# Attention with the value products of each block in two parts of 256 query columns, one per step, buffers zeroed by VectorE and GpSimd, and no loops

## Chip, cores, metric

One core of one Trainium2 chip. The metric is the device time of one execution in microseconds (us); the median of several timed runs is compared. Engines are called TensorE (PE, its weight loads PEld), VectorE (DVE), ScalarE (ACT), GpSimd (POOL) and SyncE (SP, which issues DMAs).

## The reference

Two blocks over 8 x 1024 tokens of width 256, each `x = x + s * silu(g)` with `s` and `g` computed from a layer norm of `x`. The first is a state-space scan with a small fp8 product, the second a gated delta rule and a mixture of experts whose input is an attention. The change touches only that attention (16 heads of 8 features, each batch of 1024 tokens by itself):

```python
Q = (hs @ q_w + q_b).reshape(B, S, H, HD).transpose(0, 2, 1, 3)
K = (hs @ k_w + k_b).reshape(B, S, H, KPH).transpose(0, 2, 1, 3)
V = (hs @ v_w + v_b).reshape(B, S, H, KPH).transpose(0, 2, 1, 3)
scores = jnp.einsum('bhsk,bhtk->bhst', Q[..., :KPH], K) / math.sqrt(KPH)
attn = jax.nn.softmax(scores, axis=-1)
ao = jnp.einsum('bhst,bhtv->bhsv', attn, V)
```

## The kernel before

The program is a row of phases, each with its own buffers and its own instruction streams per engine: `ssm_inputs`, `ssm_scan`, `ssm_output`, `delta_inputs`, `delta_invert`, `delta_chunks`, `attention`, `experts`. A phase starts when the one before has ended. Only `attention` (line 2090) is changed.

The work of `attention` is cut into 32 units (`UNITS`), one for each batch `b` and each set `j` of four heads. A unit does three things for its four heads:

- maxima (`maxima`, line 2254): queries times keys with 128 queries on the partitions and 1024 keys in the free dimension, as two matmuls of 512 columns into one of two PSUM tiles `psM`. VectorE reduces each tile to minus its row maximum (`maximum`, L2395). There are 32 such tiles in a unit (`MT`). When they are there, `minus_max` (L2404, L2406) splits the maxima into a head and a rest, `turn` (L2273) transposes them on TensorE, ScalarE copies them to `topT` (L2355), and SyncE writes them by DMA into two more rows of the queries (`maxima_rows`, L2167). So the scores come out with the maximum already subtracted.
- scores (`scores`, L2280): the other way round, 128 keys on the partitions and 512 queries in the free dimension, 64 per unit (`BANKS`), each into one of three PSUM banks `psS`. ScalarE takes the exponential of each (`exponentials`, L2363) into a ring `probs` of 24 slots. A score waits until the exponential three entries earlier is done (`free`).
- values (`values`, L2293): for each 128 keys of the four heads one block of four products, 32 columns of the array each, 128 keys x 512 queries, all in fp32 and added up in one PSUM bank `psV` over the eight key tiles of a half of the queries. Each product shows as two load and two matmul records, so a block is eight of each. There are 16 blocks (`GROUPS`) per unit. VectorE copies `psV` out after eight of them (`collect`, L2411), and SyncE stores the sums.

TensorE's stream is written out by hand in steps; a unit has 32 (`step`). A step issues, in this order, the first half of a maxima tile, a score, the second half of the tile, a score. The maxima are those of the tile 8 steps ahead (`LEAD`) in the next unit. After every odd step `s` the whole block `s // 2 - 1` of values follows (`sequence`); two steps and their block are called a group here. Maxima and scores of one step use opposite halves of the array's rows. After score 52 (`TURN`) comes the transpose for the next unit. The TensorE, ScalarE and VectorE streams are already without loops; SyncE runs batches 0 to 6 in one loop, GpSimd batches 1 to 7.

At the start of the phase VectorE sets `ones` to one and then zeroes, for j = 0 to 3, `k4[j]` and `q4[j]`, then `top2`, before it takes up any maximum. SyncE loads unit j (17 DMAs) when its two buffers are zeroed, and after each the rows of ones. GpSimd sets `zeros` (of `Cleared`, which clears a table for a later phase), makes the identity and fills `v4`. TensorE then makes the 32 maxima tiles of unit 0 and 8 of unit 1 before the first step.

Of the kernel before, what the change touches and what calls it, by code (L numbers as in the profile page):

```python
# [2089 lines left out]
def attention(nc, A):  # L2090
# [18 lines left out]
    SLOTS, RING = 66, 24  # L2109


    at_slot = [n if n <= TURN else n + 1 for n in range(BANKS)]
    turn_entry = TURN + 1
    bank_at = dict(zip(at_slot, range(BANKS)))
    NE = BANKS + 1
    OPEN = 4
    COLLECTED = (18 + LEAD, FIRST + LEAD)
    with ExitStack() as ctx:
# [13 lines left out]
        ident_made, ready_made, filled = m.sem("ident_made"), m.sem("ready_made"), m.sem("filled")  # L2132
# [15 lines left out]
        with nc.Block() as block:  # L2148
            @block.sync
            def _(sp):  # L2150
# [10 lines left out]
                def maxima_rows(u, j, b):  # L2161

                    sp.wait_ge(act_done, u * NE + (turn_entry + 2 - NE) if not isinstance(u, int) or u else 1)
# [5 lines left out]
                def store(u, j, b, half):  # L2169
# [13 lines left out]
                maxima_rows(0, 0, 0)  # L2183

                def sequence(b, final):
                    for j in range(NQ):
                        u = b * NQ + j
                        store(u, j, b, 0)
                        if not (final and j == NQ - 1):
                            maxima_rows(u + 1, (j + 1) % NQ, b + (j + 1) // NQ)  # L2190
                        store(u, j, b, 1)
                        if not final:
                            load(b + 1, j)
                            cleared.store(sp, u)
# [11 lines left out]
            def _(pool):  # L2206
                cleared.make(pool)
# [3 lines left out]
                                   pattern=[[-1, P]], channel_multiplier=1).then_inc(ident_made, 1)  # L2211
                for j in range(NQ):
# [4 lines left out]

                def spread_values(b, j):
                    pool.wait_ge(loaded[j], b * 16 * LOADS + 16 * LOADS)
                    m.settle(pool)  # L2220
                    pool.tensor_copy(v4[j][:, :, :, 0:HD], vraw[j][:].rearrange("p c (h r) -> p c h r", r=HD)).then_inc(v_ready, 1)  # L2221

                for j in range(NQ):
                    spread_values(0, j)
                with pool.Fori(1, B) as b:
                    for j in range(NQ):
                        pool.wait_ge(summed, b * NQ * GROUPS + (j + 2 - NQ) * GROUPS)
                        spread_values(b, j)

            def slot(j, v):  # L2230
                return (j * SLOTS + v) % RING

            def steps():

                for s in range(FIRST, BANKS // 2 + FIRST):
                    yield s, s % (BANKS // 2), s // (BANKS // 2)

            @block.tensor
            def _(pe):
# [6 lines left out]
                def maxima(u, j, t, half):  # L2246

                    h, c = tile_of(t)
                    if half == 0:
                        if t > 1:  # L2250
                            pe.wait_ge(maxed, u * MT + (t - 1))
                        elif not isinstance(u, int) or u:
                            pe.wait_ge(maxed, u * MT + t - 1)
# [6 lines left out]
                def free(u, v):  # L2260
                    if v >= 3:
                        pe.wait_ge(act_done, u * NE + (v - 1))
# [989 lines left out]
```

## Time and profile before

| | us |
|---|---|
| median of 3 timed runs (lowest to highest) | 4021.08 (4018.24 to 4024.04) |
| the profiled execution | 3990.48 |
| its span, first to last instruction | 3988.9 |
| TensorE matmuls busy | 3377.5 |
| VectorE busy | 3155.0 |
| ScalarE busy | 2370.5 |
| GpSimd busy | 1366.7 |

The costliest groups of the page belong to the attention: 1024 maxima reductions on VectorE (L2395, 1205.1 us busy), 2048 exponentials (L2363, 1061.0 us), 2048 scores (L2280, 803.4 us), 2048 maxima matmuls (L2254, 704.9 us) and 4096 records of value matmuls (L2293, 546.3 us). The attention lies between about 1850 and 3276 us of the span. Busy times of different engines overlap. Those of TensorE hold modelled ends of matmuls. Idle time stands in brackets behind an instruction, with what released it; where several conditions had to be met, the one named is the last that the profile saw. In the order of time an entry "x4" merges neighbours of one kind on one engine.

### The profile page before, as it was taken

The page shows a single profiled execution, that of the slowest core. Times are in us where ns is not written, and L with a number is a line of the kernel's source. Part 1 is how long each engine was busy: PE and PEld are TensorE (multiplying, and loading weights), DVE is VectorE, ACT ScalarE, POOL GpSimd, SP SyncE. Part 2 cuts the span into 40 slices and gives each one's busy share as a digit, 9 for nine tenths or more (in the row PEclk, how much of TensorE's full clock was granted, in tenths as well). Part 3 has the DMA queues.
Part 4 walks back from the last instruction along what each step waited for, and adds up shares of the span by engine and source line. Part 5 has one row for each costly group of instructions (what it writes and reads, how often), then busy time and mean ns, then how long its engine had stood idle before and what let it go on. Part 6 is the DMA issues. An engine that isn't in the chain of part 4 may idle for free. (4 is left out here: it accounts for less than half of the span.)

```text
span 3988.9 us, 64991 instructions
## 1 busy us (share of the span) xinstructions
PE 3377.5 (85%) x19711; PEld 2058.5 (52%) x19712; DVE 3155.0 (79%) x4214; ACT 2370.5 (59%) x4325; POOL 1366.7 (34%) x953
## 2 busy tenths in 40 slices
PE   8969898996669799797999999999999976299950
PEld 6745455553458688795333333333333324189940
DVE  7869999997866566477899999999999935277868
ACT  6668888886955433210577777777777761033323
POOL 7859998994014454301000000000000005744520
PEclk9989999998889899997799999999999996599975
DMA  7854444544869632394122323223223115222258
GB/s 262 283 187 164 159 163 166 179 146 166 280 174 255 164 111 74 109 291 134 27 54 62 69 53 72 58 55 75 54 60 71 30 21 178 87 86 89 90 175 293
DMA packets 531451, 521.11 MB, mean 131 GB/s; under 512 B 84784, under 2 KB 441264, under 8 KB 531040
## 3 DMA queue, kind: packets, MB, share of 16 engines
q1 hardware_dynamic: 517248, 480.45, 41.0%
q0 software_dynamic: 13952, 37.74, 2.7%
q8 instruction: 106, 1.74, 0.2%
q14 instruction: 145, 1.19, 0.1%
HBM read 301.15 MB, written 215.71 MB: 130 GB/s over the span
## 5 line engine op out<-in xcount | busy, mean ns | idle before, releaser
L2395 DVE TENSOR_REDUCE at_top<-at_psM 128x1 f32<-128x1024 f32 x1024 | 1205.1, 1218 | 101.5 <-PE at_psM L2254 99.8
L2363 ACT ACTIVATE at_probs<-at_psS 128x512 f32<-128x512 f32 x2048 | 1061.0, 603 | 286.0 <-PE at_psS L2280 286.0
L2280 PE MATMUL at_psS<-at_q,at_k 64*128 64x512 f32 x2048 | 803.4, 471 | 8.2 <-ACT at_probs L2363 8.1
L2254 PE MATMUL at_psM<-at_k,at_q 62*128 62x512 f32 x2048 | 704.9, 454 | 41.3 <-DMA at_vraw<-scratch_vf 22.0
L655 POOL TENSOR_TENSOR sc_prod<-sc_state,sc_c_row 128x1024 f32<-128x1024 f32 x256 | 648.8, 2564 | 84.1 <-DVE sc_state L806 72.2
L2254 PEld LDWEIGHTS at_psM<-at_k,at_q 62*128 62x128 f32 x2048 | 313.1, 190 | 621.4 <-DVE at_top L2395 539.3
L806 DVE TENSOR_TENSOR_SCAN sc_state<-sc_dec,sc_psI 128x1024 f32<-128x1024 f32 x256 | 574.2, 2276 | 43.6 <-PE sc_psI L727 34.0
L2293 PE MATMUL at_psV<-at_probs,at_v 128*32 128x512 f32 x4096 | 546.3, 605 | 0.0
L738 PE MATMUL sc_psY<-sc_prod,sc_ident 128*128 128x512 f32 x1024 | 480.5, 599 | 15.2 <-DVE sc_y L792 15.2
L2221 POOL COPY at_v<-at_vraw 128x256 f32<-128x256 f32 x32 | 12.8, 401 | 1249.4 <-DMA at_vraw<-scratch_vf 1166.6
L2280 PEld LDWEIGHTS at_psS<-at_q,at_k 64*128 64x128 f32 x2048 | 337.7, 184 | 170.3 <-ACT at_probs L2363 160.4
L674 ACT ACTIVATE sc_scaled<-sc_uT,sc_b_col 128x256 f32<-128x256 f32 x768 | 325.2, 494 | 96.3 <-PE sc_psI L727 96.3
L688 ACT ACTIVATE sc_dec<-sc_dt,sc_a_exp 128x1024 f32<-128x1024 f32 x256 | 285.3, 1136 | 7.4 <-DVE sc_state L806 7.4
L727 PEld LDWEIGHTS sc_psI<-sc_ident,sc_scaled 128*128 128x128 f32 x1536 | 180.9, 144 | 177.0 <-DVE sc_state L806 82.8
L738 PEld LDWEIGHTS sc_psY<-sc_prod,sc_ident 128*128 128x128 f32 x1024 | 179.7, 192 | 167.1 <-issue 142.2
L727 PE MATMUL sc_psI<-sc_ident,sc_scaled 128*128 128x128 f32 x1536 | 207.9, 280 | 58.6 <-DVE sc_state L806 51.0
L2884 POOL DMA_INDIRECT scratch_ys<-ex_y,ex_slot x156 | 170.3, 1092 | 184.8 <-DVE ex_y L3017 137.5
L2438 PEld LDWEIGHTS ex_psY<-ek_w,ex_hid 128*128 128x128 f32 x1872 | 223.8, 188 | 3.2 <-issue 0.3
L2438 PE MATMUL ex_psY<-ek_w,ex_hid 128*128 x1872 | 224.9, 279 | 0.0
L2904 ACT ACTIVATE ex_xT<-ex_psT 128x512 fp32r<-128x512 f32 x39 | 23.3, 598 | 266.4 <-PE ex_psT L2934 266.4
L2580 POOL DMA_INDIRECT scratch_xs<-er_rows,ek_spot x128 | 130.5, 1019 | 74.5 <-issue 41.3
L2293 PEld LDWEIGHTS at_psV<-at_probs,at_v 128*32 128x32 f32 x4096 | 80.6, 108 | 128.4 <-ACT at_probs L2363 94.1
(409 smaller groups left out, 4904.4 us busy)
## 6 DMA issues: line engine op xcount, KB each, us to landing
sc_c_row<-scratch_bc SPq DMA_DIRECT2D x128, 512.0 KB, 3.7
scratch_xs<-at_zeros SPq DMA_DIRECT2D x140, 264.0 KB, 4.7
sc_b_row<-scratch_bc SPq DMA_DIRECT2D x32, 512.0 KB, 5.0
ec_y<-scratch_ys SPq DMA_DIRECT2D x32, 512.0 KB, 6.1
ex_x<-scratch_xs SPq DMA_DIRECT2D x39, 264.0 KB, 3.3
si_x<-in_x SPq DMA_DIRECT2D x16, 512.0 KB, 5.6
scratch_xn<-si_xn SPq DMA_DIRECT2D x16, 512.0 KB, 6.2
scratch_x_t<-si_xT SPq DMA_DIRECT2D x16, 512.0 KB, 3.1
```

The source lines that it names most:

```text
L655: pool.tensor_tensor(prod[:, (n * H + h) % 8, :], state[slot][:], c_row[n % ROWS][:], ALU.mult).then_inc(prod_ready, 1)
L674: act.activation(scaled[DIAG.index(n) % 2][:, c, :, :], uT[k][:, c, :, :], ACT.Copy, scale=b_col[:, bass.ds(b * CHUNKS + c, 1), n]).then_i ...
L688: act.activation(dec[slot][:], dt[k][h][:], ACT.Exp, scale=a_exp[:, h, n:n + 1]).then_inc(dec_ready, 1)
L727: last = pe.transpose(psI[h][:, c, :], scaled[order % 2][:, c, h, :], ident[:])
L738: last = pe.matmul(psY[h][:, cols], ident[:], prod[:, own % 8, cols], start=(n == 0), stop=(n == S - 1))
L806: dve.tensor_tensor_scan(state[slot][:], dec[slot][:], psI[h][:].rearrange("p c t -> p (c t)"), 0.0, ALU.mult, ALU.add).then_inc(state_rea ...
L2254: ins = pe.matmul(psM[t % 2][:, half * TILE:(half + 1) * TILE], rows_of(q4[j], h, 0, MAXROW)[:, c * P:(c + 1) * P], rows_of(k4[j], h, 0, M ...
L2280: pe.matmul(psS[v % 3][:], rows_of(k4[j], h, 0, GROUP)[:, c * P:(c + 1) * P], rows_of(q4[j], h, 0, GROUP)[:, half * TILE:(half + 1) * TILE ...
L2293: last = pe.matmul(psV[32 * h:32 * h + 32, :], v4[j][:, c, h, :], probs[:, slot(j, at_slot[4 * g + n]), :], start=(c == 0), stop=(c == KC ...
L2363: act.activation(probs[:, slot(j, v), :], psS[v % 3][:], ACT.Exp).then_inc(act_done, 1)
L2395: dve.tensor_reduce(top[j % 2][:, h, c:c + 1], psM[t % 2][:], AX.X, ALU.max, negate=True).then_inc(maxed, 1)
L2438: last = pe.matmul(out, a, b, start=start and n == 0, stop=stop and n == len(parts) - 1)
```

## The change

Value products: `values` now takes a group number and a part. Part 0 is query columns 0 to 255 of the block, part 1 columns 256 to 511. After an odd step comes part 0 of the block whose turn it is, after the even step behind it part 1. For the last block of each half (`last_keys`) both parts come after the odd step. The flag that starts an accumulation is set only on part 0 of the first key tile, for both parts lie in the same bank. Only part 1 tells ScalarE and VectorE that the block is done.

Zeroing: VectorE zeroes `k4`, `q4` of units 0 and 1, then sets `ones` and `top2`, and waits for `top2` alone; GpSimd zeroes those of units 2 and 3 first, and `zeros` is set after the first four `spread_values`. The loads wait for `zeroed[j]` only; the rows of ones are stored after all four loads.

No loops: SyncE's and GpSimd's batches are written out, and entries of the score banks are numbered once over all units (`score_at`, `turn_at`); bank and ring slot follow from that number.

```diff
-    SLOTS, RING = 66, 24
+    RING, PART = 24, TILE // 2
+    score_at, turn_at, entries = {}, {}, 0
+    turn_at[0], entries = entries, entries + 1
+    for u in range(UNITS):
+        for s in range(MT):
+            for n in (2 * s, 2 * s + 1):
+                score_at[u, n], entries = entries, entries + 1
+                if n == TURN and u + 1 < UNITS:
+                    turn_at[u + 1], entries = entries, entries + 1
...
                 for j in range(NQ):
-                    sp.wait_ge(ready_made, 2 * j + 3)
+                    sp.wait_ge(zeroed[j], 2)
                     m.settle(sp)
                     load(0, j)
+                sp.wait_ge(ones_made, 1)
+                m.settle(sp)
+                for j in range(NQ):
                     for group in range(2):
                         dst = k4[j][GROUP * group + MAXROW:GROUP * (group + 1), :, :].bitcast(F32)
                         sp.dma_start(dst, ones[:]).then_inc(ones_in, 16)
...
-                with sp.Fori(0, B - 1) as b:
-                    sequence(b, False)
-                sequence(B - 1, True)
+                for u in range(UNITS):
+                    store(u, 0)
+                    if u + 1 < UNITS:
+                        maxima_rows(u + 1)
+                    store(u, 1)
+                    if u + NQ < UNITS:
+                        load(u // NQ + 1, u % NQ)
+                        cleared.store(sp, u)
...
             def _(pool):
-                cleared.make(pool)
+                for j in range(2, NQ):
+                    pool.memset(k4[j][:].bitcast(F32), 0.0).then_inc(zeroed[j], 1)
+                    pool.memset(q4[j][:].bitcast(F32), 0.0).then_inc(zeroed[j], 1)
...
                 for j in range(NQ):
                     spread_values(0, j)
-                with pool.Fori(1, B) as b:
+                cleared.make(pool)
+                for b in range(1, B):
...
-                def values(u, j, g):
+                def values(group, part):
 
-                    half, c = g // KC, g % KC
-                    pe.wait_ge(act_done, u * NE + (at_slot[4 * g + 3] + 2))
-                    if c == 0:
-                        pe.wait_ge(sums_ready, u * NHALF + (half + 1))
-                    if g == 0:
-                        pe.wait_ge(v_ready, u + (2 * NQ + 1))
+                    u, g = group // GROUPS, group % GROUPS
+                    j, half, c = u % NQ, g // KC, g % KC
+                    cols = slice(part * PART, (part + 1) * PART)
+                    if part == 0:
+                        pe.wait_ge(act_done, score_at[u, 4 * g + 3] + 1)
+                        if c == 0:
+                            pe.wait_ge(sums_ready, u * NHALF + (half + 1))
+                        if g == 0:
+                            pe.wait_ge(v_ready, u + (2 * NQ + 1))
                     for n, h in enumerate(KEYED):
-                        last = pe.matmul(psV[32 * h:32 * h + 32, :], v4[j][:, c, h, :], probs[:, slot(j, at_slot[4 * g + n]), :],
-                                         start=(c == 0), stop=(c == KC - 1))
-                    last.then_inc(summed, 1)
+                        last = pe.matmul(psV[32 * h:32 * h + 32, cols], v4[j][:, c, h, :], probs[:, slot(u, 4 * g + n), cols],
+                                         start=(c == 0 and part == 0), stop=(c == KC - 1 and part == 1))
+                    if part == 1:
+                        last.then_inc(summed, 1)
+
+                def values_after(at):
+
+                    group = (at - 3) // 2
+                    if group < 0:
+                        return
+                    last_keys = group % KC == KC - 1
+                    if at % 2:
+                        values(group, 0)
+                    if at % 2 == 0 and not last_keys or at % 2 and last_keys:
+                        values(group, 1)
...
+                for u in range(UNITS):
+                    for s in range(MT):
+                        if u and s == 0:
+                            pe.wait_ge(top_in[u % NQ], (u // NQ + 1) * 16 * QUAD)
+                        step(u, s)
+                        values_after(u * MT + s)
+                for at in range(UNITS * MT, UNITS * MT + 2):
+                    values_after(at)
...
             def _(dve):
-                dve.memset(ones[:], 1.0).then_inc(ready_made, 1)
-                for j in range(NQ):
-                    dve.memset(k4[j][:].bitcast(F32), 0.0).then_inc(ready_made, 1)
-                    dve.memset(q4[j][:].bitcast(F32), 0.0).then_inc(ready_made, 1)
-                dve.memset(top2[:], 0.0).then_inc(ready_made, 1)
+                for j in range(2):
+                    dve.memset(k4[j][:].bitcast(F32), 0.0).then_inc(zeroed[j], 1)
+                    dve.memset(q4[j][:].bitcast(F32), 0.0).then_inc(zeroed[j], 1)
+                dve.memset(ones[:], 1.0).then_inc(ones_made, 1)
+                dve.memset(top2[:], 0.0).then_inc(top2_made, 1)
```

## Rows read from the trace of the kernel before

**Rows 1.** Table by stage: stretch, length, busy time per engine (instructions), TensorE clock, DMA.
```profile
1960.00:3200.00 1240.00, 1233.61 (x7582) 446.03 (x7582) 1149.82 (x1064) 981.70 (x1918) 11.22 (x28) 1.00 0.26 60
```

**Rows 2.** Order of time, one group: start us, us, engine, line, operation, [idle before].
```profile
2401.40 0.50 PE L2280 MATMUL at_psS<-at_q,at_k 64*128 64x512 f32 x1
...
2401.73 0.73 PE L2280 MATMUL at_psS<-at_q,at_k 64*128 64x512 f32 x2
2401.93 2.06 ACT L2363 ACTIVATE at_probs<-at_psS 128x512 f32<-128x512 f32 x4 [0.55 <-PE at_psS L2280]
...
2401.97 0.72 PE L2254 MATMUL at_psM<-at_k,at_q 62*128 62x512 f32 x2
...
2402.16 2.36 DVE L2395 TENSOR_REDUCE at_top<-at_psM 128x1 f32<-128x1024 f32 x2 [0.25 <-PE at_psM L2254]
...
2402.58 0.18 PEld L2280 LDWEIGHTS at_psS<-at_q,at_k 64*128 64x128 f32 x1 [0.33 <-ACT at_probs L2363]
...
2403.01 0.16 PEld L2293 LDWEIGHTS at_psV<-at_probs,at_v 128*32 128x32 f32 x8 [0.25 <-ACT at_probs L2363]
...
2404.01 0.49 PE L2280 MATMUL at_psS<-at_q,at_k 64*128 64x512 f32 x1
```

**Rows 3.** Groups by line: count, busy us, mean ns, idle before (1900 to 3300 us).
```profile
L2363 ACT ACTIVATE at_probs<-at_psS 128x512 f32<-128x512 f32 x2048 | 1061.0, 603 | 286.0 <-PE at_psS L2280 286.0
```

**Rows 4.** Order of time, last unit, TensorE: two groups in a row.
```profile
3249.78 0.73 PE L2280 MATMUL at_psS<-at_q,at_k 64*128 64x512 f32 x3
...
3252.38 0.73 PE L2280 MATMUL at_psS<-at_q,at_k 64*128 64x512 f32 x3
```

**Rows 5.** Line 2273, the transposes: duration min/median/max, first and last start.
```profile
L2273 PE MATMUL at_psS<-at_ident,at_top x32: 328/329/332, 1962.9 to 3265.8; 128*128 128x128 f32 x32
```

**Rows 6.** Line 2293, the value products: loads and matmuls, min/median/max ns.
```profile
L2293 PEld LDWEIGHTS at_psV<-at_probs,at_v x4096: 106/109/151, 1931.4 to 3273.5; 128*32 128x32 f32 x196
L2293 PE MATMUL at_psV<-at_probs,at_v x4096: 592/617/1061, 1931.4 to 3274.0; 128*32 128x512 f32 x196
```

**Rows 7.** Line 1997 of an earlier stage: loads and matmuls of 256 columns.
```profile
L1997 PEld LDWEIGHTS dc_psOut<-dc_wo,dc_og x128: 186/190/190, 1704.8 to 1845.3; 128*128 128x128 f32 x128
L1997 PE MATMUL dc_psOut<-dc_wo,dc_og x128: 379/379/483, 1704.8 to 1845.5; 128*128 128x256 f32 x128
```

**Rows 8.** Order of time, earlier stage: line 1997, eight matmuls in one row.
```profile
1797.53 1.99 PE L1997 MATMUL dc_psOut<-dc_wo,dc_og 128*128 128x256 f32 x8
```

**Rows 9.** Order of time, the step with the transpose.
```profile
2424.91 0.50 PE L2280 MATMUL at_psS<-at_q,at_k 64*128 64x512 f32 x1
...
2425.34 0.33 PE L2273 MATMUL at_psS<-at_ident,at_top 128*128 128x128 f32 x1
...
2425.60 0.49 PE L2254 MATMUL at_psM<-at_k,at_q 62*128 62x512 f32 x1
...
2426.44 0.39 PE L2280 MATMUL at_psS<-at_q,at_k 64*128 64x512 f32 x1
2426.76 0.16 PEld L2293 LDWEIGHTS at_psV<-at_probs,at_v 128*32 128x32 f32 x8 [0.31 <-ACT at_probs L2363]
```

**Rows 10.** Order of time, the start of the attention.
```profile
1853.32 1.76 DVE L2386 MEMSET at_ones<- 2x2048 f32 x1 [6.10 <-PEq L3207]
...
1855.46 1.76 DVE L2388 MEMSET at_k<- 128x2048 f32 x1 [0.38 <-issue]
...
1858.03 0.95 POOL L2213 MEMSET at_v<- 128x1024 f32 x1
...
1859.47 0.36 SPq L2156 DMA_DIRECT2D at_q<-scratch_qs  x1
...
1867.86 0.53 PEld L2254 LDWEIGHTS at_psM<-at_k,at_q 62*128 62x128 f32 x4 [22.36 <-issue]
...
1872.39 2.36 DVE L2395 TENSOR_REDUCE at_top<-at_psM 128x1 f32<-128x1024 f32 x2
...
1926.56 0.79 PE L2254 MATMUL at_psM<-at_k,at_q 62*128 62x512 f32 x1 [4.33 <-DMA at_q<-at_topT]
```

More of the change, by code:

```diff
@@ L2244, in tile_of, with maxima @@
                     return HEADS[t % QUAD], t // QUAD
[L2246 to L2253, printed above, removed]
+                def maxima(u, t, half):
+                    j, (h, c) = u % NQ, tile_of(t)
+                    if half == 0 and u * MT + t > 1:
+                        pe.wait_ge(maxed, u * MT + t - 1)
                     ins = pe.matmul(psM[t % 2][:, half * TILE:(half + 1) * TILE],
@@ L2258, in maxima @@
                         ins.then_inc(scored, 1)
-                def free(u, v):
-                    if v >= 3:
-                        pe.wait_ge(act_done, u * NE + (v - 1))
-                    elif v < 2 and (not isinstance(u, int) or u):
-                        pe.wait_ge(act_done, u * NE + v)
-                    elif isinstance(u, int) and not u:
-                        pe.wait_ge(act_done, 1)
-                def turn(u, needed):
-                    free(u, turn_entry)
-                    if needed:
-                        top_at.wait(pe, u + 1, "rest")
-                    pe.transpose(psS[turn_entry % 3][:, 0:P], top2[:], ident[:]).then_inc(keyed, 1)
@@ L2275, in scores, with free, turn @@
-                def scores(u, j, n):
+                def free(e):
+                    if e >= 3:
+                        pe.wait_ge(act_done, e - 2)
+                def turn(u):
+                    e = turn_at[u]
+                    free(e)
+                    top_at.wait(pe, u, "rest")
+                    pe.transpose(psS[e % 3][:, 0:P], top2[:], ident[:]).then_inc(keyed, 1)
+                def scores(u, n):
+                    j, e = u % NQ, score_at[u, n]
                     half, c, h = n // (KC * QUAD), n // QUAD % KC, KEYED[n % QUAD]
-                    v = at_slot[n]
-                    free(u, v)
-                    pe.matmul(psS[v % 3][:], rows_of(k4[j], h, 0, GROUP)[:, c * P:(c + 1) * P],
+                    free(e)
+                    pe.matmul(psS[e % 3][:], rows_of(k4[j], h, 0, GROUP)[:, c * P:(c + 1) * P],
@@ L2313, in _ @@
-                pe.wait_ge(loaded[0], 16 * LOADS)
-                for t in range(MT):
-                    for half in range(NHALF):
-                        maxima(0, 0, t, half)
-                pe.wait_ge(loaded[1], 16 * LOADS)
-                for t in range(LEAD):
-                    for half in range(NHALF):
-                        maxima(1, 1, t, half)
-                top_at.wait(pe, 0, "rest")
-                pe.transpose(psS[2][:, 0:P], top2[:], ident[:]).then_inc(keyed, 1)
+                        scores(u, n)
@@ L2323, in _ @@
+                        if n == TURN and u + 1 < UNITS:
+                            turn(u + 1)
+                for u, count in ((0, MT), (1, LEAD)):
+                    pe.wait_ge(loaded[u], 16 * LOADS)
+                    for t in range(count):
+                        for half in range(NHALF):
+                            maxima(u, t, half)
+                turn(0)
                 pe.wait_ge(top_in[0], 16 * QUAD)
                 pe.wait_ge(ones_in, 2 * 16 * NQ)
-                for s in range(FIRST):
-                    step(0, 0, 0, s, False, False)
@@ L2377, in _, with turned @@
[L2377 to L2382 removed]
+                def turned(u):
+                    e = turn_at[u]
+                    act.wait_ge(keyed, e + 1)
+                    act.activation(topT[:], psS[e % 3][:, 0:P], ACT.Copy).then_inc(act_done, 1)
@@ new lines, in exponential @@
+                def exponential(u, n):
+                    e, at = score_at[u, n], u * BANKS + n
+                    act.wait_ge(keyed, e + 1)
+                    if at >= RING:
+                        act.wait_ge(summed, (at - RING) // QUAD + 1 + GROUPS)
+                    act.activation(probs[:, slot(u, n), :], psS[e % 3][:], ACT.Exp).then_inc(act_done, 1)
+                turned(0)
+                for u in range(UNITS):
+                    for s in range(MT):
+                        for n in (2 * s, 2 * s + 1):
+                            exponential(u, n)
+                            if n == TURN and u + 1 < UNITS:
+                                turned(u + 1)
```

137 lines of the change are left out of this document (35 added, 102 removed).

## The prediction

> **What bounds the kernel now.** I read the views from the outside in. The stage table says where the attention stands: between 1960 and 3200 us TensorE is busy for 1233.6 of 1240 us, VectorE for 1149.8, ScalarE for 981.7, at full granted clock [rows 1]. A busy TensorE proves little, because the ends of its matmuls are modelled and pairs that wait look busy, and VectorE is nearly as full. So I went to the order of time within one group, which is two steps: four pairs of matmuls (maxima and scores on opposite halves of the array's rows, so they run together), then one block of value products.
>
> The group's first score starts at 2401.40, that of the next at 2404.01: 2.61 us [rows 2]. In between the last of the four scores waits until 2402.58, and the releaser named is ScalarE. The chain that fixes the period: first score at 1.40; its exponential at 1.93, 0.53 later; it takes 0.60 [rows 3]; 0.05 later, at 2.58, the score starts that needs this same bank (there are three); the value block follows 0.43 later, at 3.01; it holds TensorE for 1.00, and at 4.01 the next group starts [rows 2]. 0.53 + 0.60 + 0.05 + 0.43 + 1.00 = 2.61. VectorE idles 0.25 per period, ScalarE 0.55, because the long block keeps new scores away [rows 2]. That VectorE is not the limit shows in the last unit: it has no maxima at all, and its period is still 2.60 (3249.78 to 3252.38) [rows 4]. A whole unit of 16 groups takes (3265.8 - 1962.9)/31 = 42.03 us, from the first and the last of the 32 transposes [rows 5].
>
> **The change: the value products.** Each block is cut into 256 columns at the odd step and 256 at the next even step, except the last block of each half (2 of 16), which stays whole so that its sum is collected at the same step. The number of instructions of line 2293 doubles from 4096 to 8192, with the same number of columns.
>
> What is a half block worth? A whole one holds TensorE for 4.01 - 3.01 = 1.00 [rows 2], in two rounds of four matmuls side by side. The shortest matmul of 512 columns there takes 592 ns [rows 6]; one of the same type with 256 columns, on line 1997, takes 379 [rows 7]. So 256 columns less save 213 ns: the stream scales, the rest (about 0.17) is latency. A half block saves 0.213 in each of its two rounds: 1.00 - 0.43 = 0.57. Its lower bound is 0.50, if everything scaled. Its upper bound: each round's weight load stands bare, 0.109 more per half block, [rows 6], thus 0.68. I take 0.57, for line 1997 runs eight 256-column matmuls, each with a load of 190 ns [rows 7], in 1.99 us, so (1.99 - 0.38)/7 = 0.23 apart [rows 8]: loads longer than these hide under the same stream.
>
> The step then runs: first pair at 0, second pair 0.33 later (1.40 to 1.73) [rows 2]; from the second pair, when it did not wait, to the first load of the block 0.32 (2426.44 to 2426.76, the one place where a block follows an unstalled score) [rows 9]; half block 0.57. Sum 1.22 to 1.23 a step, 2.45 a group. Are the waits gone? First score of a step to its exponential's end 1.13, plus 0.05: 1.18 after it the next step's second score may start, and it is due at 1.22 + 0.33 = 1.55. The loop of before with the half block is 1.18 + 0.43 + 0.57 = 2.18 for two steps, below 2.45. ScalarE wants two exponentials, 0.52 each when they follow one another (2.06 for four): 1.03 a step. VectorE wants at most 1.18 (2.36 for two); a maximum starts 0.43 behind its second matmul (1.73 to 2.16), so at 0.76 in its step, and frees its bank at about 2.0, which the step two on needs at 2.44 [rows 2]. So every wait has cover, the thinnest 0.04 a step on VectorE, and what is late next is TensorE itself: the forecast is a step bound by the array.
>
> The two whole blocks: second pair at 0.33, block from 0.65 to 1.65, then a step with no block (0.33 + 0.23, as from 1.73 to 1.97 [rows 2]), next pair at 2.21; its second score waits for the exponential of the step before: 1.65 + 1.18 = 2.83 instead of 2.55, and the following block then starts at 3.26. From block to block 2.61, as before. The transpose of line 2273 takes 0.43 behind the first pair and 0.26 ahead of the second (2424.91, 2425.34, 2425.60) [rows 9], and the block then comes 0.43 after that fresh pair: 1.12 where a plain step has 0.65, so 0.47. Before, the group with the transpose took 0.24 more, since part of it lay in the waits.
>
> Unit: 14 x 2.45 + 2 x 2.61 + 0.47 = 40.0 us against 42.03, so 2.0 less; for 32 units (the last has the same chain) 65 us. With the ends for the half block: 0.50 would give 28 x 0.07 = 2 us more per unit but then VectorE is the limit, and its busy time is 1149.8/1240 x 42.03 = 39.0 per unit [rows 1], so at most 1 us more, 32 in all; 0.68 would cost 28 x 0.11 = 3.1 per unit, 99 in all.
>
> **The change: the start of the stage.** VectorE now zeroes two buffers' pairs instead of four; GpSimd the others; the ones come after. Before: the ones (1853.32, 1.76) stood ahead of the first pair, so SyncE issued its first load at 1859.47 and the first maxima matmul ran at 1867.86; and VectorE took up the maxima only at 1872.39, behind ten memsets [rows 10]. One memset with its gap is 2.15 (1853.32 to 1855.46). Now the first load starts 2.15 earlier, the first matmul at 1865.7, and VectorE is free at 1872.4 - 4 x 2.15 = 1863.8, so the first maximum waits for the matmuls: some 0.9 behind the first, an estimate from the 0.79 of one at this low clock (at 1926.56), at 1866.6: 5.8 us earlier [rows 10]. Behind it the chain is as before, 40 maxima. GpSimd's four memsets, at twice 0.95 for twice the columns, last until about 1861; the identity follows, before 1865; the value buffers, needed after 1930, come behind it. That both engines write at once costs nothing: VectorE's memset takes 1.76 while GpSimd writes too [rows 10]. The last two loads wait on GpSimd, but SyncE first issues the two groups ahead of them, 17 issues of 0.36 each, so it comes to them at about 1857.3 + 12.3 = 1869.6.
>
> **The change: no loops.** Only SyncE and GpSimd had loops. Their work has cover: at the start TensorE waits 4.33 us from the transpose until the rows of topT have landed (1926.56) [rows 10], and within the units the transpose comes 5 steps and 1.7 us, that is 7.8 us, ahead of need. I cost it at nothing, with 0 to 2 us either way; if that cover were gone each of the 31 units would wait.
>
> **Sum.** 65 + 5.8 = 71 us. The profiled execution took 3990.5 us with a span of 3988.9; the median of the timed runs, 4021.1, is 0.8% above it. The same 71 us are taken off the median: 3950.
>
> **A rule against it.** The trace shows all eight weight loads of a block within 0.16 us [rows 2], while the first round's matmuls, 617 ns long in the median, are running [rows 6]. The Trainium skill (TensorE: Matmul & The Clock Gate, Part 3, what overlaps and what doesn't) says a weight load overlaps a running matmul only when the row groups differ; here every value product uses all rows, so by it the second round's loads would stand bare in each half block. The trace of before disagrees. It is the mechanism of the first rival.
>
> **The rivals.** (1) Slower: the fixed part of a half block is larger than scaling says, because the second round's loads no longer hide, at 0.109 [rows 6]. Then a step is 0.65 + 0.68 = 1.335 and a unit 28 x 1.335 + 5.22 + 0.47 = 43.07: 1.04 x 32 = 33 slower, less 5.8 at the start, 4048. It decides from a half block of 0.65 on, where a unit is 42.0 again; my 0.57 is only 0.08 below. For it: the margin is thin and is paid 896 times. Against: line 1997's spacing. Chance 0.08. (2) No change in the steps: TensorE still waits for an exponential or a maximum once per group and 2.61 stays; only the start gains: 4015. For it: three banks are few. Against: the covers above, and the last unit, where only ScalarE's loop is left. Chance 0.07. (3) Part of the gain: VectorE, which will be busy 39 of 40 us, falls behind after each collection of psV (twice a unit) and at the two subtractions, and TensorE, in order, waits; up to 0.4 each time, 1 us a unit, 32 in all: 3965 to 3985. Chance 0.13. (4) VectorE's bound is reached, the steps being shorter than I add up: 3915 to 3925. Chance 0.05. The forecast keeps 0.67, from 3930 to 3965.
>
> The range holds the forecast and (3), with the little of (4) that lies above its lower end: 3925 to 3985, 0.80. A measurement of this kernel tells about 0.2% (8 us) from no change. Faster by more than that: the forecast, (3), (4), and 0.02 of (2), where the waits shrink by a little, 0.87 in all; within it the rest of (2), 0.05; slower (1), 0.08.
>
> **What would show it.** Right: 128x256 matmuls of the value line at about 379 ns in the second round; steps of 1.22 us from maxima pair to maxima pair; transposes 40.0 us apart; ScalarE's idle time ahead of the exponentials cut to half or less; TensorE's waits for ScalarE only behind the whole blocks; the first maximum near 1866.6. Wrong: half blocks over 0.65 (rival 1), maxima waits of TensorE that last over 0.3 us beyond the block (rival 3), or a group of 2.61 with a wait for ScalarE in it (rival 2).

## The result, and the profile after

| | before | after |
|---|---|---|
| median of the timed runs, us | 4020.51 (4 runs, 4018.24 to 4024.04) | 3953.51 (4 runs, 3952.32 to 3954.11) |
| ratio, 95% interval | | 0.9832 [0.9815, 0.9849] |
| span of the profiled execution, us | 3988.9 | 3952.5 |

The median fell by 67 us. The prediction was 3950 us, 71 less than the median that it started from.

Table by stage, the kernel after: stretch, length, then busy time (instructions) of PE, PEld, DVE, ACT, POOL, TensorE's granted clock, DMA share, GB/s.

```profile
1970.00:3150.00 1180.00, 1179.99 (x11319) 455.13 (x11321) 1168.64 (x1058) 1022.36 (x1911) 11.27 (x28) 1.00 0.28 63
```

VectorE was busy for 92.7% of the stage [rows 1]; it is now for 99.0%. That number alone would say that VectorE is the bound, and experiment 6 shows that it isn't. VectorE's busy time reads high: the record of one maximum lasts 1.22 us, but two in a row take 2.36 [rows 2], so the next can begin 1.14 us behind the one before it.

Order of time in the kernel after, two plain steps; it answers to [rows 2].

```profile
2400.95 0.49 PE L2251 MATMUL at_psM<-at_k,at_q 62*128 62x512 f32 x1
2400.95 0.18 PEld L2273 LDWEIGHTS at_psS<-at_q,at_k 64*128 64x128 f32 x1
2400.95 0.49 PE L2273 MATMUL at_psS<-at_q,at_k 64*128 64x512 f32 x1
...
2401.28 0.39 PE L2251 MATMUL at_psM<-at_k,at_q 62*128 62x512 f32 x1
2401.29 0.39 PE L2273 MATMUL at_psS<-at_q,at_k 64*128 64x512 f32 x1
2401.49 2.32 ACT L2353 ACTIVATE at_probs<-at_psS 128x512 f32<-128x512 f32 x4 [0.37 <-PE at_psS L2273]
2401.61 0.16 PEld L2289 LDWEIGHTS at_psV<-at_probs,at_v 128*32 128x32 f32 x8 [0.36 <-issue]
2401.61 0.64 PE L2289 MATMUL at_psV<-at_probs,at_v 128*32 128x256 f32 x8
2402.18 0.18 PEld L2251 LDWEIGHTS at_psM<-at_k,at_q 62*128 62x128 f32 x1 [0.41 <-DVE at_top L2375]
2402.18 0.49 PE L2251 MATMUL at_psM<-at_k,at_q 62*128 62x512 f32 x1
...
2402.52 0.39 PE L2273 MATMUL at_psS<-at_q,at_k 64*128 64x512 f32 x1
2402.84 0.16 PEld L2289 LDWEIGHTS at_psV<-at_probs,at_v 128*32 128x32 f32 x8 [0.36 <-issue]
```

No score waits here any more. The step is 2402.18 - 2400.95 = 1.23: 0.34 from one score to the next (2401.29), 0.32 to the block, 0.57 for the half block. The wait for VectorE that the row at 2402.18 names is idle time of the weight loads while the half block's matmuls still ran. With maxima half as long (experiment 6) the same gap of 0.41 stands at the same place, so VectorE doesn't make it.

The places where something still waits are the groups with a whole block. Order of time in the kernel after, behind such a block:

```profile
2410.00 0.50 PE L2273 MATMUL at_psS<-at_q,at_k 64*128 64x512 f32 x1
2410.24 0.68 DVE L2389 COPY at_sums<-at_psV 128x512 f32<-128x512 f32 x1
...
2411.18 0.18 PEld L2273 LDWEIGHTS at_psS<-at_q,at_k 64*128 64x128 f32 x1 [0.42 <-ACT at_probs L2353]
...
2411.61 0.64 PE L2289 MATMUL at_psV<-at_probs,at_v 128*32 128x256 f32 x8
```

From the first score behind the whole block (2410.00) to the one that waits (2411.18) it is 1.18, the 0.53 + 0.60 + 0.05 of the prediction. Between 1970 and 3150 us a score's load waited for an exponential 58 times, which is twice a unit, once for each whole block.

Groups by line in the kernel after (mean ns; idle time and what ended it):

```profile
L2375 DVE TENSOR_REDUCE at_top<-at_psM 128x1 f32<-128x1024 f32 x1024 | 1229.4, 1222 | 22.1 <-PE at_psM L2251 19.1
L2353 ACT ACTIVATE at_probs<-at_psS 128x512 f32<-128x512 f32 x2048 | 1108.9, 596 | 177.4 <-PE at_psS L2273 54.8
```

The value products in the kernel after (duration min/median/max, first and last start), to set beside [rows 6]:

```profile
L2289 PE MATMUL at_psV<-at_probs,at_v x8192: 379/379/634, 1928.9 to 3210.8; 128*32 128x256 f32 x200
```

ScalarE idled 286.0 us ahead of its exponentials [rows 3], now 177.4, of which the view puts 54.8 down to a score. The matmuls of 256 columns take 379 ns, as line 1997's did [rows 7].

The transposes within the units, first and last start (this answers to [rows 5]):

```profile
L2266 PE MATMUL at_psS<-at_ident,at_top x31: 328/329/331, 1958.0 to 3162.6; 128*128 128x128 f32 x31
```

A unit takes (3162.6 - 1958.0)/30 = 40.15 us, against 42.03. The difference times 32 is 60 us.

The start of the stage in the kernel after, order of time (answers to [rows 10]):

```profile
1855.96 1.76 DVE L2366 MEMSET at_k<- 128x2048 f32 x1 [6.13 <-PEq L3181]
...
1859.97 0.36 SPq L2160 DMA_DIRECT2D at_q<-scratch_qs  x1
...
1868.57 0.53 PEld L2251 LDWEIGHTS at_psM<-at_k,at_q 62*128 62x128 f32 x4 [20.46 <-issue]
...
1869.90 1.23 DVE L2375 TENSOR_REDUCE at_top<-at_psM 128x1 f32<-128x1024 f32 x1 [3.48 <-PE at_psM L2251]
```

From VectorE's first memset to its first maximum it was 1872.39 - 1853.32 = 19.07 us, now 13.94: 5.1 less. With the units that makes 65 us, and the timed medians differ by 67.

The two profiled executions differ by 36 us only, for a reason outside the attention. In the execution profiled before, the phase behind it (routing and the experts' products) ran from 3291.1 to 3852.7; in the one after, from 3227.8 to 3816.2: 561.6 and 588.4 us. The row of an early and of a late instruction, first of before, then of after:

```profile
L2708 DVE TENSOR_SCALAR er_obw<-er_ones,er_ob x2: 279/279/279, 3291.1 to 3291.3; 128x128 f32<-128x128 f32 x2
L3146 DVE SCALAR_TENSOR_TENSOR ec_shift<-ec_known x1: 226/226/226, 3852.7 to 3852.7; 128x64 f32<-128x64 f32 x1
```

```profile
L2682 DVE TENSOR_SCALAR er_obw<-er_ones,er_ob x2: 281/281/281, 3227.8 to 3228.0; 128x128 f32<-128x128 f32 x2
L3120 DVE SCALAR_TENSOR_TENSOR ec_shift<-ec_known x1: 226/226/226, 3816.2 to 3816.2; 128x64 f32<-128x64 f32 x1
```

The eleven runs below have edits in the attention only, and in their profiled executions this stretch took 585.0 to 597.4 us (597.4, from 3277.8 to 3875.2, in `before_max_half`, which is the kernel before with one edit). So the execution of the kernel before that was profiled was 23 to 36 us short there, and it lay 28 us below the fastest timed run of its kernel (3990.5 against 4018.2). Below, kernels are compared by their units and stages where a single execution is all there is.

### The profile page after: what moved, and what is told of

It reads as the page before. It is cut to its first block and busy times, and to the rows that moved or that the text cites. A ratio compares the mean times of both kernels' runs of the same rounds, so it can differ in the third digit from the quotient of the medians.

```text
span 3952.5 us, 71732 instructions
## 1 busy us (share of the span) xinstructions
PE 3330.8 (84%) x23806; PEld 2070.5 (52%) x23807; DVE 3174.8 (80%) x4210; ACT 2420.0 (61%) x4324; POOL 1370.9 (35%) x957
## 5 line engine op out<-in xcount | busy, mean ns | idle before, releaser
L2375 DVE TENSOR_REDUCE at_top<-at_psM 128x1 f32<-128x1024 f32 x1024 | 1229.4, 1222 | 22.1 <-PE at_psM L2251 19.1
L2353 ACT ACTIVATE at_probs<-at_psS 128x512 f32<-128x512 f32 x2048 | 1108.9, 596 | 177.4 <-PE at_psS L2273 54.8
L2251 PE MATMUL at_psM<-at_k,at_q 62*128 62x512 f32 x2048 | 756.1, 453 | 29.6 <-DMA at_vraw<-scratch_vf 20.1
L2273 PE MATMUL at_psS<-at_q,at_k 64*128 64x512 f32 x2048 | 756.5, 446 | 0.9 <-ACT at_probs L2353 0.9
L2289 PE MATMUL at_psV<-at_probs,at_v 128*32 128x256 f32 x8192 | 641.2, 390 | 0.0
L2289 PEld LDWEIGHTS at_psV<-at_probs,at_v 128*32 128x32 f32 x8192 | 167.8, 108 | 349.1 <-issue 175.5
L2273 PEld LDWEIGHTS at_psS<-at_q,at_k 64*128 64x128 f32 x2048 | 309.0, 185 | 43.7 <-ACT at_probs L2353 42.5
```

What stands on the lines that cost most here:

```text
L2251: ins = pe.matmul(psM[t % 2][:, half * TILE:(half + 1) * TILE], rows_of(q4[j], h, 0, MAXROW)[:, c * P:(c + 1) * P], rows_of(k4[j], h, 0, M ...
L2273: pe.matmul(psS[e % 3][:], rows_of(k4[j], h, 0, GROUP)[:, c * P:(c + 1) * P], rows_of(q4[j], h, 0, GROUP)[:, half * TILE:(half + 1) * TILE ...
L2289: last = pe.matmul(psV[32 * h:32 * h + 32, cols], v4[j][:, c, h, :], probs[:, slot(u, 4 * g + n), cols], start=(c == 0 and part == 0), sto ...
L2353: act.activation(probs[:, slot(u, n), :], psS[e % 3][:], ACT.Exp).then_inc(act_done, 1)
L2375: dve.tensor_reduce(at, psM[t % 2][:], AX.X, ALU.max, negate=True).then_inc(maxed, 1)
```

## The experiments

My theory: before, a group lasts as long as the chain of its first score, that score's exponential, the fourth score that needs the bank, and the whole block (2.61 us). Half blocks shorten the chain below TensorE's own work, and TensorE's own work sets the step after. The rivals: VectorE is the bound before or after; narrow matmuls or straight code bring the gain; the narrow matmuls cost bare weight loads.

**1. The block whole again, everything else kept** (`whole_odd`).

```diff
-    RING, PART = 24, TILE // 2
+    RING, PART = 24, TILE
...
-                                         start=(c == 0 and part == 0), stop=(c == KC - 1 and part == 1))
-                    if part == 1:
-                        last.then_inc(summed, 1)
+                                         start=(c == 0), stop=(c == KC - 1))
+                    last.then_inc(summed, 1)
...
                     if at % 2:
                         values(group, 0)
-                    if at % 2 == 0 and not last_keys or at % 2 and last_keys:
-                        values(group, 1)
```

> The changed kernel, but each block whole (512 columns) behind the odd step, as before; zeroing and straight code stay. My theory: the chain first score, exponential, fourth score, block returns, with a group of 2.61 us and transposes 42.0 us apart; only the start of the stage gains, some 5 us: 4015 us, ratio to before 0.999. Rival (straight code on SyncE and GpSimd brought part of the gain): 3955 to 4000.

Measured: 4016.7 us, ratio 0.9984 [0.9975, 0.9994]. Its transposes:

```profile
L2266 PE MATMUL at_psS<-at_ident,at_top x31: 327/328/332, 1957.3 to 3218.3; 128*128 128x128 f32 x31
```

(3218.3 - 1957.3)/30 = 42.03 us a unit, as before. What is left is the start: from VectorE's first memset to its first maximum it takes 1867.02 - 1853.02 = 14.00 us, as in the change. The written-out loops bring nothing in the units; nearly all of the gain is in the value products.

**2. Both halves behind the odd step** (`two_parts_odd`): as narrow and as many as in the change, but not moved.

```diff
                     if at % 2:
                         values(group, 0)
-                    if at % 2 == 0 and not last_keys or at % 2 and last_keys:
                         values(group, 1)
```

> The changed kernel with both halves of each block behind the odd step, so the matmuls are as narrow and as many as in the change, but not moved. My theory: what pays is that a block no longer stands in one piece ahead of the next scores; two halves together take 1.00 to 1.02 us, so a group 2.61 to 2.63 us: 4015 to 4025. Rival (narrow matmuls are better by themselves): near 3953. Rival (each narrow round costs something): 1024 more rounds at 0.109 at most, 4100 or more.

Measured: 4017.9 us, ratio 0.9993 [0.9983, 1.0003]; a unit takes (3220.6 - 1956.5)/30 = 42.14 us.

```profile
L2266 PE MATMUL at_psS<-at_ident,at_top x31: 327/328/332, 1956.5 to 3220.6; 128*128 128x128 f32 x31
```

Narrowness brings nothing by itself and costs 0.1 us a unit. What pays is the place of the second half.

**3. The zeroing as before** (`old_zeroing`).

```diff
-                for j in range(2):
+                dve.memset(ones[:], 1.0).then_inc(ones_made, 1)
+                for j in range(NQ):
                     dve.memset(k4[j][:].bitcast(F32), 0.0).then_inc(zeroed[j], 1)
                     dve.memset(q4[j][:].bitcast(F32), 0.0).then_inc(zeroed[j], 1)
-                dve.memset(ones[:], 1.0).then_inc(ones_made, 1)
```

and without GpSimd's four memsets.

> The changed kernel with the zeroing as before: VectorE sets ones and then all eight buffers. My theory: steps unchanged (transposes 40.15 us apart), the first maximum some 5 us later, so 3958 us. Rival (the zeroing is covered anyway): 3953.

Measured: 3960.5 us, ratio 0.9842 [0.9826, 0.9859]. The intervals overlap, so the ratios can't tell this from the change's 0.9832. The trace can: from VectorE's first memset to its first maximum it takes 1872.12 - 1853.06 = 19.06 us, 5.1 more than in the change, and the units last (3165.6 - 1961.0)/30 = 40.15, as there. Both parts of the new zeroing are undone at once here; what each is worth was not tried.

```profile
1853.06 1.76 DVE L2362 MEMSET at_ones<- 2x2048 f32 x1 [6.11 <-PEq L3178]
...
1872.12 2.36 DVE L2372 TENSOR_REDUCE at_top<-at_psM 128x1 f32<-128x1024 f32 x2
```

**4. The kernel before with half of each exponential** (`before_exp_half`).

```diff
-                    act.activation(probs[:, slot(j, v), :], psS[v % 3][:], ACT.Exp).then_inc(act_done, 1)
+                    act.activation(probs[:, slot(j, v), 0:TILE // 2], psS[v % 3][:, 0:TILE // 2], ACT.Exp).then_inc(act_done, 1)
...
                 dve.memset(top2[:], 0.0).then_inc(ready_made, 1)
+                dve.memset(probs[:, :, TILE // 2:], 1.0).then_inc(ready_made, 1)
```

> The kernel before, with each exponential taken over 256 of its 512 columns (the other half of each slot is set to one at the start, which costs VectorE some 5 us, so the values of half of the queries are left out). My theory: the exponential is in the chain of 2.61 us, so a group gets shorter by what the exponential does, 0.2 us, until VectorE binds at 2.36: 2.40 us, unit 38.6, in all 110 us less (3915). Rival (TensorE's amount of work or VectorE is the bound before): group stays at 2.61, 4025.

Measured: 3963.2 us, beside 4023.4 for the kernel before, where I had expected 3915; a unit takes (3203.6 - 1965.3)/31 = 39.94. Order of time, one plain group, then a later place where VectorE copies `psV` out:

```profile
2400.07 0.49 PE L2280 MATMUL at_psS<-at_q,at_k 64*128 64x512 f32 x1
...
2400.60 1.36 ACT L2363 ACTIVATE at_probs<-at_psS 128x256 f32<-128x256 f32 x4 [1.00 <-PE at_psS L2280]
...
2401.03 0.18 PEld L2280 LDWEIGHTS at_psS<-at_q,at_k 64*128 64x128 f32 x1
...
2402.47 0.50 PE L2280 MATMUL at_psS<-at_q,at_k 64*128 64x512 f32 x1
...
2415.62 0.68 DVE L2412 COPY at_sums<-at_psV 128x512 f32<-128x512 f32 x1
...
2416.42 0.16 PEld L2293 LDWEIGHTS at_psV<-at_probs,at_v 128*32 128x32 f32 x8 [0.24 <-ACT at_probs L2363]
...
2419.28 0.16 PEld L2293 LDWEIGHTS at_psV<-at_probs,at_v 128*32 128x32 f32 x8 [0.37 <-issue]
```

A plain group lasts 2402.47 - 2400.07 = 2.40 us. The chain with the exponential now 0.38 says the same: 0.53 + 0.38 + 0.05 + 0.43 + 1.00 = 2.39. ScalarE's work was far from full in the kernel before (981.7 of 1240 us [rows 1]), and yet a shorter exponential shortens the group. The unit did not become 38.6. With groups of 2.40, VectorE, which needs 2.28 for two maxima that follow one another at 1.14, has little time to catch up after its two copies of `psV` and its subtractions, and TensorE waits for it: from block to block behind the copy it is 2419.28 - 2416.42 = 2.86 us. I had left those out.

**5. The kernel before with half of each maximum** (`before_max_half`).

```diff
-                    dve.tensor_reduce(top[j % 2][:, h, c:c + 1], psM[t % 2][:], AX.X, ALU.max, negate=True).then_inc(maxed, 1)
+                    dve.tensor_reduce(top[j % 2][:, h, c:c + 1], psM[t % 2][:, 0:TILE], AX.X, ALU.max, negate=True).then_inc(maxed, 1)
```

> The kernel before, with each maximum over 512 of the 1024 keys. My theory: VectorE was not the bound, so a group stays at 2.61 and a unit at 42.0; the 40 maxima before the first step save some 12 us, as they did in the changed kernel, 4009 in all. Rival (VectorE's 0.25 idle per group was its own doing): a unit of 40 or less.

Measured: 4012.9 us beside 4022.5; a unit takes (3252.7 - 1951.4)/31 = 41.98.

```profile
L2273 PE MATMUL at_psS<-at_ident,at_top x32: 328/329/332, 1951.4 to 3252.7; 128*128 128x128 f32 x32
```

VectorE, busy for 93% of the stage, was not the bound before.

**6. The changed kernel with half of each maximum** (`after_max_half`), by the same edit.

> The changed kernel, with each maximum taken over 512 of the 1024 keys (any value near the maximum serves the softmax, so this leaves out half of VectorE's work and little else). My theory: a step of 1.23 us is TensorE's own (pair 0.33, second pair to block 0.32, half block 0.57), so transposes stay 40.15 us apart; only the 40 maxima before the first step get faster, some 20 us: 3933. Rival (VectorE, busy 39 of 40 us, holds TensorE back): transposes nearer than 39.5.

Measured: 3949.4 us beside 4021.5; a unit takes (3149.2 - 1944.4)/30 = 40.16.

```profile
L2266 PE MATMUL at_psS<-at_ident,at_top x31: 328/329/331, 1944.4 to 3149.2; 128*128 128x128 f32 x31
```

and one maximum in the order of time:

```profile
2399.46 0.69 DVE L2375 TENSOR_REDUCE at_top<-at_psM 128x1 f32<-128x512 f32 x1 [0.90 <-PE at_psM L2251]
```

VectorE's maxima take 0.69 and it now idles between them, and the unit moves by no more than a hundredth. So VectorE doesn't set the step, and with experiment 7, where ScalarE doesn't either, TensorE's own work is left. I had expected 3933. From VectorE's first memset to the first transpose of the units it takes 1944.4 - 1854.8 = 89.6 us, against 1958.0 - 1856.0 = 102.0 in the change: the start gained 12 us and not my 20. The granted clock is 0.50 there, and VectorE now waits for the matmuls of each two tiles, which come 2.00 us apart where two maxima took 2.36:

```profile
1886.62 1.29 DVE L2375 TENSOR_REDUCE at_top<-at_psM 128x1 f32<-128x512 f32 x2 [0.71 <-PE at_psM L2251]
1888.62 1.29 DVE L2375 TENSOR_REDUCE at_top<-at_psM 128x1 f32<-128x512 f32 x2 [0.71 <-PE at_psM L2251]
```

Of these 12 us 7 were lost again in the phase behind the attention (595.7 us here, 588.4 in the change's execution).

**7. The changed kernel with half of each exponential** (`after_exp_half`), the edit of experiment 4.

> The changed kernel, with each exponential taken over 256 of its 512 columns (values of half of the queries left out; setting the other half to one costs some 5 us at the start). My theory: the plain steps stay at 1.23; only behind the two whole blocks of a unit does a score wait for an exponential, so each of these groups goes from 2.62 to about 2.45 and a unit from 40.15 to 39.8: 3947. Rival (the exponential is still in the chain of every group, as before, where the same edit took 0.21 off each): unit 37 to 38.

Measured: 3956.5 us beside 4021.5; a unit takes (3159.9 - 1959.9)/30 = 40.00 instead of 40.15. The same edit that took 2.1 us from a unit before takes 0.15 after: the exponential is out of the chain everywhere but behind the whole blocks. There it gave 0.08 each where I had said 0.17. The group itself fell to 2.41 us from block to block (2409.21 to 2411.62), but the step behind it took 1.36 and not 1.23, since its maxima wait for VectorE, which works off maxima without a pause behind its copy of `psV`:

```profile
2411.05 5.74 DVE L2376 TENSOR_REDUCE at_top<-at_psM 128x1 f32<-128x1024 f32 x5
...
2412.32 0.18 PEld L2251 LDWEIGHTS at_psM<-at_k,at_q 62*128 62x128 f32 x1 [0.55 <-DVE at_top L2376]
```

**8. Quarters** (`quarters`): each half block as two runs of 128 columns.

```diff
-                    for n, h in enumerate(KEYED):
-                        last = pe.matmul(psV[32 * h:32 * h + 32, cols], v4[j][:, c, h, :], probs[:, slot(u, 4 * g + n), cols],
-                                         start=(c == 0 and part == 0), stop=(c == KC - 1 and part == 1))
+                    for quarter in (2 * part, 2 * part + 1):
+                        cols = slice(quarter * P, (quarter + 1) * P)
+                        for n, h in enumerate(KEYED):
+                            last = pe.matmul(psV[32 * h:32 * h + 32, cols], v4[j][:, c, h, :], probs[:, slot(u, 4 * g + n), cols],
+                                             start=(c == 0 and quarter == 0), stop=(c == KC - 1 and quarter == 3))
```

> The changed kernel with each half block made in two runs of 128 columns: the same columns, twice as many matmuls and loads again. My theory: a matmul of 128 columns still hides the next loads (0.107 us of stream against 0.109), so a half block stays at 0.57 to 0.62: unit 40.2 to 41.5, 3955 to 3995. Rival (my first in the prediction: loads stand bare as the matmuls get shorter): 0.109 for each of two more rounds, step 1.45, unit 46, 4140.

Measured: 3966.8 us beside 4021.5; a unit takes (3168.3 - 1957.3)/30 = 40.37, that is 0.21 more, or 8 ns for each of its 28 half blocks. Two of its rows, a block and the pair behind it:

```profile
2402.00 0.64 PE L2290 MATMUL at_psV<-at_probs,at_v 128*32 128x128 f32 x16
2402.57 0.50 PE L2251 MATMUL at_psM<-at_k,at_q 62*128 62x512 f32 x1
```

Sixteen matmuls of 128 columns hold TensorE for 0.57 us, as eight of 256 do. The loads stay hidden even here. Of the 13 us between 3966.8 and 3953.5 the units make 7. The phase behind the attention took 594.1 us here and 588.4 in the change's execution, which is most of the rest.

**9. Parted by heads** (`by_heads`): two heads at all 512 columns in each part.

```diff
-                    for n, h in enumerate(KEYED):
-                        last = pe.matmul(psV[32 * h:32 * h + 32, cols], v4[j][:, c, h, :], probs[:, slot(u, 4 * g + n), cols],
-                                         start=(c == 0 and part == 0), stop=(c == KC - 1 and part == 1))
+                    for n, h in list(enumerate(KEYED))[2 * part:2 * part + 2]:
+                        last = pe.matmul(psV[32 * h:32 * h + 32, :], v4[j][:, c, h, :], probs[:, slot(u, 4 * g + n), :],
+                                         start=(c == 0), stop=(c == KC - 1))
```

> The changed kernel with the blocks parted by heads, not by queries: two heads at 512 columns in each part, so as many matmuls as before in all. My theory: four heads run side by side, and two take as long as four, so a part holds TensorE for 1.00 and not for 0.57: step 1.65, unit near 54, 4390 us. Rival (any part of half the products takes half the time, so that spreading alone pays): step 1.23, 3953.

Measured: 4324.1 us beside 4021.5; a unit takes (3516.3 - 1965.1)/30 = 51.71.

```profile
2400.14 1.05 PE L2289 MATMUL at_psV<-at_probs,at_v 128*32 128x512 f32 x4
2401.12 0.49 PE L2251 MATMUL at_psM<-at_k,at_q 62*128 62x512 f32 x1
```

Two heads hold TensorE for 0.98 us, as long as four do, because the four run side by side. The step is 1.64, where I had said 1.65. A group with a whole block takes 2.61 as elsewhere; my unit of 54 had given each of the two 1 us more.

**10. Values in bfloat16, parted and whole** (`bf16_values` on the change, `bf16_whole` on experiment 1).

```diff
-        v4 = [m.sb(f"v4{j}", [P, KC, QUAD, 32]) for j in range(NQ)]
+        v4 = [m.sb(f"v4{j}", [P, KC, QUAD, 32], BF16) for j in range(NQ)]
...
-        probs = m.sb("probs", [P, RING, TILE])
+        probs = m.sb("probs", [P, RING, TILE], BF16)
```

> The changed kernel with the exponentials and the values in bfloat16 (less exact: the value products are made once instead of in two rounds, at one column per cycle). My theory: TensorE's step falls below VectorE's, half block 0.25 and step 0.90, so VectorE binds: 32 maxima at 1.14, two copies and the two subtractions, 38.1 to 38.6 us a unit, 3890 to 3905. Rival (TensorE's fixed times or ScalarE at 1.03 a step hold it): unit 39 or more.

> As bf16_values, but with each block whole behind the odd step, as before the change. My theory: a whole block is then 0.36 long, the chain first score, exponential, fourth score, block takes 0.53 + 0.60 + 0.05 + 0.43 + 0.36 = 1.97, less than VectorE's 2.36, so parting the block brings nothing more: within 5 us of bf16_values. Rival (parting is worth 66 us by itself): 3950 or more.

Measured: parted 3942.6 us, ratio 0.9804 [0.9766, 0.9843]; whole 3904.6 us, ratio 0.9719 [0.9695, 0.9744]. I had expected 3890 to 3905 for the parted version and the whole one within 5 us of it. So parting does not just bring nothing here, it costs 38 us, which neither side had foreseen. Tables by stage, parted; the first three are stretches of different granted clock, the last is the stage:

```profile
1966.50:1986.90 20.40, 16.56 (x144) 6.95 (x142) 20.40 (x20) 19.03 (x36) 0.40 (x1) 1.00 0.54 122
1986.90:2007.30 20.40, 20.40 (x109) 8.81 (x109) 16.95 (x17) 14.63 (x28) 0.00 (x0) 0.50 0.01 3
2027.90:2034.70 6.80, 6.78 (x36) 2.95 (x36) 6.03 (x7) 4.85 (x10) 0.00 (x0) 0.50 0.05 11
1950.00:3150.00 1200.00, 1019.97 (x7744) 432.03 (x7743) 1153.16 (x1084) 1050.57 (x1963) 11.27 (x28) 0.89 0.27 62
```

and the stage of the whole version:

```profile
1950.00:3100.00 1150.00, 893.52 (x5770) 361.60 (x5768) 1134.05 (x1077) 1037.40 (x1943) 11.21 (x28) 0.97 0.27 64
```

At full clock VectorE binds, busy for 20.40 of 20.40 us with 20 instructions; TensorE idles a fifth of the time. After such a stretch its granted clock is 0.50, here for 20 us, the 1.2 GHz level, and then TensorE is busy all the time and gets through 109 matmul records where there were 144. From the first transpose of the units to the last, the parted version has 35 such slow stretches, most of them under 7 us, 251 us in all; the whole version has 15, 58 us in all. An estimate from these rows: 193 us more at the low level, with a quarter less done (109 for 144), cost some 47 us, so the clock is enough to explain the 38. In the parted version the stage's mean clock is 0.89, in the whole version 0.97; a unit takes 39.75 and 38.47 us. Why the parted version has more of the slow stretches is not settled: it spreads the same columns over more and shorter pauses, but no run separates the two, and it is the whole version whose TensorE is idle more (893.5 of 1150 us busy against 1020.0 of 1200). The mechanism expected (VectorE becomes the bound near 38.1 to 38.6 us a unit) shows in the whole version. The rival for the parted one (39 us or more) had the size right and the reason wrong: it named TensorE's fixed times or ScalarE.

`bf16_whole` is faster than both kernels, by the ratios some 45 us below the change. It is less exact in the exponentials and values, so it trades exactness for time, which the change does not.

## Why the prediction was right

- The bound of before: right. The chain of 2.61 us is confirmed by experiment 4, where a group went to 2.40 as the exponential got shorter. That VectorE was not the bound is confirmed by experiment 5.
- A half block 0.57: measured 0.57. The 592 to 379 ns scaling and line 1997's spacing carried it. Rival 1 (bare loads, 0.109 for each half block) fell; experiment 8 shows loads hidden even at 128 columns: all eight loads of a half block issue within 0.16 us, and two more rounds cost 8 ns and not 218. The Trainium skill (TensorE: Matmul & The Clock Gate, Part 3) says that a load overlaps running matmuls only when the row groups differ; this case's trace goes against it. The same Part also names loads into the background weight buffer as ones that are pulled ahead; no run here tells whether these were such.
- The step 1.22 to 1.23: measured 1.23. Whole-block groups 2.61: measured (40.15 - 28 x 1.23 - 0.47)/2 = 2.62. The transpose's step: the pair 0.26 behind it and the block 0.43 behind that pair, as taken (below).
- A unit 40.0: measured 40.15. Nearly all of the 0.15 is the rounding of the step, 1.23 instead of 1.225, over 28 steps.
- The units in sum 65: measured 60, for the same reason. The start 5.8: measured 5.1. Counted from VectorE's first memset, the first maxima matmul came 1.9 us earlier (12.61 for 14.54), not 2.15, and the first maximum 1.3 behind it, not 0.9. No loops, nothing: `whole_odd` leaves no room for more.
- The sum 71: the timed medians give 67. That I took the 71 off the median and not off the profiled time mattered more than any term, and the prediction gives no reason for it. The profiled execution of before was 23 to 36 us short in another phase; 71 off its 3990.5 would have said 3919.5. That the total came out so close owes something to this choice.
- Rival 2 (no change in the steps) and rival 4 (VectorE's bound) fell. Rival 3 (VectorE falls behind, up to 1 us a unit) was close, since two maxima in a row took 2.36 us and two steps take 2.46, but by experiment 6 it costs nothing.
- One sign that was named did not come. ScalarE's idle time ahead of the exponentials was to fall to half or less; it fell from 286.0 to 177.4 us. The prediction's own sum says so: 1.03 us of exponentials in a step of 1.23 leave 0.20, times 896 plain steps 179 us.

Order of time in the kernel after, TensorE around a transpose, to set beside [rows 9]:

```profile
2399.69 0.33 PE L2266 MATMUL at_psS<-at_ident,at_top 128*128 128x128 f32 x1
2399.95 0.50 PE L2251 MATMUL at_psM<-at_k,at_q 62*128 62x512 f32 x1
...
2400.38 0.64 PE L2289 MATMUL at_psV<-at_probs,at_v 128*32 128x256 f32 x8
```

## What to carry to other kernels

Where three short buffers stand between two engines, look for the chain that goes once around them, and add up whether a long block on the producer lies in it: its busy engines may all have slack, and yet the period is fixed. Parting such a block pays only if the parts shrink in time (fewer columns; not fewer heads that ran side by side anyway), if they are put in different steps, and if the period is really set by that chain: with bfloat16 values it was not, and parting cost 38 us. The fixed cost of each part (here 0.14 of the 0.57 us, what is left beyond two rounds of 0.213) must also stay below the wait that it removes; that is reasoned, no run varies it. And compare stages, not spans, when a single profiled execution differs from the timed runs.

## What was not expected of the hardware

- With bfloat16 values TensorE is busy for about four fifths of the time at full clock, and its granted clock falls to 0.50 again and again: 35 stretches and a mean of 0.89 in the parted version, 15 and 0.97 in the whole one, which is 38 us faster with the same columns and is idle more. So the idle share alone does not decide it. In the two fp32 kernels the clock stays at 1.00 in the attention's units. Less work for TensorE made the parted bfloat16 kernel no faster than the fp32 one beyond noise (0.9804 against 0.9832, the intervals overlap).
- The phase behind the attention takes between 561.6 and 597.4 us in thirteen profiled executions, with the same code; all but the lowest lie between 585.0 and 597.4. What decides it stays open.
